# Edge attention on one core: the chain of maxima moved behind queries and sums in TensorE's order, scaling and merging one turn later

## What is computed

```python
k, q, v = ...                                   # per node, 4 heads of 64
score = sum(q_att[etype, col] * k[row], -1)     # per edge and head
m = segment_max(score, col)                     # over the edges into a node
ex = exp(score - m[col])
denom = segment_sum(ex, col)
agg = segment_sum(ex / denom[col] * msg[row], col)
```

## Time and profile before

| | us |
|---|---|
| median of 3 runs (7957.71 to 7974.63) | 7957.74 |
| the profiled execution | 7995.27 |
| its span | 7993.2 |
| mean granted PE clock, share of full | 0.75 |
| edge part of the first layer, first queries to last scaling | 816.8 to 2453.8 |
| edge part of the last layer, the same | 6073.4 to 7780.4 |

### The profile page before, as it was taken

The page is one execution under the profiler, slowest core; times in us unless marked ns, Lnnn a source line. Parts: engine busy times, 40 slices in busy tenths (PEclk is TensorE's granted clock), DMA queues, the critical chain, the costliest instruction groups (busy, mean ns, idle before and its releaser), DMA issues. The chain is left out here.

```text
span 7993.2 us, 97165 instructions
## 1 busy us (share of the span) xinstructions
PE 4632.6 (58%) x25691; PEld 3338.9 (42%) x25691; DVE 3629.8 (45%) x7669; ACT 2265.8 (28%) x7764; POOL 3116.6 (39%) x3162
## 2 busy tenths in 40 slices
PE   1698477777776404444445532885265666666664
PEld 1465355454455303333333322775122555555542
DVE  8111566666664341121111220111324878888875
ACT  0233355555453210000001110221011444444450
POOL 0320566666660026666662001001103555556540
PEclk9999677777778756666765556998566888888785
DMA  3333666666662223333333114872114666666662
GB/s 108 101 126 123 193 200 199 199 196 202 199 192 68 57 74 92 94 89 94 92 92 68 28 28 137 264 262 82 58 61 141 200 194 205 202 203 200 200 154 79
DMA packets 603761, 1110.04 MB, mean 139 GB/s; under 512 B 157032, under 2 KB 416238, under 8 KB 599843
## 3 DMA queue, kind: packets, MB, share of 16 engines
q0 software_dynamic: 204144, 617.42, 27.2%
q1 hardware_dynamic: 399216, 488.05, 18.9%
HBM read 983.67 MB, written 208.59 MB: 149 GB/s over the span
## 5 line engine op out<-in xcount | busy, mean ns | idle before, releaser
L714 POOL DMA_INDIRECT l3e_kv<-t_table,k_recs x912 | 966.7, 1060 | 706.9 <-ACT l3e_vw L991 385.7
L714 POOL DMA_INDIRECT l0e_kv<-t_table,k_recs x912 | 973.5, 1067 | 650.7 <-ACT l0e_vw L991 387.2
L1370 PE MATMUL l2e_pA<-l2e_row,l2e_oh 128*128 128x257 f32 x1824 | 614.9, 505 | 954.0 <-DVE l2e_acc L1349 329.3
L1324 POOL DMA_INDIRECT l2e_row<-t_table,l2e_idx x912 | 898.2, 985 | 403.7 <-issue 268.1
L1370 PEld LDWEIGHTS l2e_pA<-l2e_row,l2e_oh 128*128 128x128 f32 x1824 | 449.7, 255 | 1118.8 <-issue 1033.3
L948 PE MATMUL l0e_pA<-l0e_vw,l0e_ohf 128*128 128x260 f32 x1824 | 653.7, 499 | 197.6 <-issue 100.8
L991 ACT ACTIVATE l3e_vw<-l3e_kv,l3e_w 128x64 f32<-128x64 f32 x2736 | 679.8, 334 | 0.1
L991 ACT ACTIVATE l0e_vw<-l0e_kv,l0e_w 128x64 f32<-128x64 f32 x2736 | 679.8, 334 | 0.0
L900 PE MATMUL l3e_pQE<-l3e_qb,l3e_ohT 128*128 128x256 bf16 x2736 | 431.4, 320 | 405.6 <-issue 377.9
L1349 DVE SCALAR_TENSOR_TENSOR l2e_acc<-l2e_acc,k_itf,l2e_pA 128x257 f32<-128x257 f32 x228 | 109.8, 482 | 1065.4 <-issue 1000.8
L948 PEld LDWEIGHTS l0e_pA<-l0e_vw,l0e_ohf 128*128 128x128 f32 x1824 | 420.2, 244 | 353.7 <-issue 166.0
(11 more groups left out here) (452 smaller groups left out, 7541.6 us busy)
## 6 DMA issues: line engine op xcount, KB each, us to landing
exp_w<-in_L_gnn_w SPq DMA_DIRECT2D x224, 512.0 KB
t_table<-l0n_tab SPq DMA_DIRECT2D x26, 2048.0 KB, 6.8
l0e_qb<-t_q SPq DMA_DIRECT2D x228, 192.0 KB
l3e_qb<-t_q SPq DMA_DIRECT2D x228, 192.0 KB
t_agg<-l0e_acc SPq DMA_DIRECT2D x228, 130.0 KB
t_agg<-l3e_acc SPq DMA_DIRECT2D x228, 130.0 KB
l0e_drow<-t_drow SPq DMA_DIRECT2D x57, 512.0 KB
l3e_drow<-t_drow SPq DMA_DIRECT2D x57, 512.0 KB
```

Of the source, the lines that this page charges most:

```text
L714: pool.indirect_dma_start(kv[:, n % SK, g, :], None, table[:, :], bass.IndirectOffsetOnAxis(ap=K["recs"][:, n, g, ridx:ridx + 1], axis=0)) ...
L1324: pool.indirect_dma_start(row[:, s, g, 0:D], None, table[:, :], bass.IndirectOffsetOnAxis(ap=idx[:, i, g:g + 1], axis=0)).then_inc(row_rea ...
L1370: last = pe.matmul(pA[s % 2][:, 0:W], oh[:, s, g, :], row[:, s, g, :], start=(g == 0), stop=(g == G - 1))
```

## The change

On PE, `shift` goes from the head of turn j = 1 to its end, `spread` from turn j = 0 to turn j = 1 behind the queries, `turn_ends` behind the sums of turn j = 0. On DVE, `candidates`, `block_max` and `node_max` stand behind the merge of turn j = 1 and not ahead of its products; `shifted` and `drop_new` go from the end of turn j = 1 to the head of turn j = 2; scaling, rescaling and merging handle items one turn older (t - 2 and t - 4). ACT copies the turned ends at the head of turn j = 1 and not within the scaling of turn j = 0, and takes the exponentials in turn j = 2. PE sums item t - 3. SP stores item n - 13 behind the queries of n. Loops run one turn longer. No instruction is added or taken away.

```diff
-                n, r, x = t + BI, t - 3, t - 1
+                n, r, x = t + BI, t - 4, t - 2
...
-                if live(m) and j == 1:
-                    candidates(m)
-                    block_max(m)
+                if live(m) and j == 2:
+                    shifted(m)
+                    drop_new(m)
                 if 0 <= r < NI:
                     rescale(r)
-                if live(m) and j == 1:
-                    node_max(m)
...
                 if live(m) and j == 1:
-                    shifted(m)
-                    drop_new(m)
+                    candidates(m)
+                    block_max(m)
+                    node_max(m)
                 if n < NI:
                     scores(n)
+                if live(m) and j == 1:
+                    drop(m)
...
+                if n + 1 < NI:
+                    queries(n + 1)
+                if live(m) and j == 1:
+                    spread(m)
+                if 0 <= t - 3 < NI:
+                    sums(t - 3)
+                if live(m) and j == 0:
+                    turn_ends(m)
                 if live(m) and j == 1:
                     shift(m)
-                if n + 1 < NI:
-                    queries(n + 1)
-                if live(m) and j == 0:
-                    turn_ends(m)
-                    spread(m)
-                if 0 <= t - 2 < NI:
-                    sums(t - 2)
```

More of the change, by code:

```diff
@@ L686, in _ @@
             load_rows(1)
-            for n in range(1, NI + 12):
+            for n in range(1, NI + 13):
                 if n < NI:
@@ L988, in weigh @@
                     act.wait_ge(a_ps, n - VS + 1)
-                for g in range(g0, g1):
+                for g in range(AW):
                     for h in range(H):
                         last = act.activation(vw[:, v, g, h, 0:DK], kv[:, n % SK, g, D + h * DK:D + (h + 1) * DK], ACT.Copy, scale=w[:, m % 2, j, g, h:h + 1])
-                if g1 == AW:
-                    last.then_inc(vwa_ready, 1)
+                last.then_inc(vwa_ready, 1)
             def turned_ends(m):
@@ L1009, in weights @@
                 act.activation(w[:, m % 2, :, :, :].rearrange("p i g h -> p (i g h)"), z[:, :], ACT.Exp).then_inc(w_ready, 1)
-            for t in range(0, NI + 1):
+            for t in range(0, NI + 2):
                 m, j = divmod(t, BI)
-                y = t - 1
+                y = t - 2
                 if live(m) and j == 1:
+                    turned_ends(m)
+                if live(m) and j == 2:
                     weights(m)
```

16 lines of the change are left out of this document (5 added, 11 removed).

## The result

The changed kernel takes 8002.32 us (median of five runs, 7993.03 to 8027.22); the kernel before takes 7957.71 beside it. The ratio is 1.0053, 95% interval 1.0041 to 1.0064: 45 us slower by the medians, where 39 us faster was forecast. The time lies in the stated range (7700 to 8020), on the wrong side of its middle. The profiled execution took 8027.22 us, 32 more than the one of before.

What follows compares the result with a forecast made beforehand. The prediction took waits to bound the kernel, chiefly for PE completions released with POOL's gather runs. Last layer -46, first layer 0, ends +7 gave 7956 for the profiled execution, 7919 for the median; range 7700 to 8020.

Steps and rivals of the forecast that it cites:

- Late completions, released with POOL's run: Likeliest case: PE's completions stay late until POOL's gather run ends; 7919 us, between 7870 and 7945, chance 0.42.
- rival 2: The lateness is a backlog of PE's real work; 108 to 214 us saved, 7811 down to 7705, chance 0.22.
- Rival 3: Completions come on time in the new order and POOL bounds; 7565 us, with half of it 7740, chance 0.10.
- First layer at 0: First layer's batch stays 28.28 us, so no gain; bounds -6.2 to +1.7 us per batch.
- The waits merely move: First layer, DVE: the wait before `l0e_z` grows, the one before the merge goes, and the batch stays 28.28 us.
- `l0e_z` to the first freed slot stays 4.35: First layer: time from `l0e_z` until scaling frees a ring slot for POOL, taken as unchanged at 4.35 us.
- The forecast sign: First layer: `l0e_z` every 28 us or so, some 2.2 us behind POOL's last gather before a 6.5 us pause.
- Last layer at -0.8: Last layer: 0.8 us saved per batch, 57 batches, 46 us; bounds 86 us saved and 23 lost.
- the walk: Last layer, one batch step by step from `l3e_ohrT`'s end: best case 27.1 against 28.66 us, at worst 0.4 worse.
- The wrong sign the prediction named: Last layer: candidates waiting over 2.4 us, or a wait before `l3e_z`, would show the forecast wrong there.
- Ends at +7: One more turn at the end of each of the two edge parts, 3.38 us each, 7 us in all.
- Rival 4: First layer: lateness fixed per completion starts later, +1.7 us per batch; 8016 with the last layer's gain, 8062 without; chance 0.18.

Runs made afterwards that it cites:

- long pauses: Kernel before, with POOL writing a 128x1024 scratch tile between one item's gathers and the next's, first layer only; 7775 us on a late chip (one run).
- short pauses: POOL writes a 128x448 scratch tile between items' gathers, both layers: kernel before with it 7852 us (0.9868), changed kernel with it 7909 us (0.9941), late chips.
- the hold: POOL holds item 4m+8's gathers until batch m's spread completes: new order 1.0063, old order (first layer only) 1.0006 on the punctual chip, 1.0092 on late ones.
- the best order: New order in the first layer's edge part alone, last layer as in the kernel before; 7906 us, ratio 0.9943 on the late chips.

## Why the prediction was wrong, point by point

**Late completions, released with POOL's run: right in kind.** The prediction's first reading holds: before, `l0e_z` came within 3 us of the end of POOL's run in 39 of 40 batches, 2.2 us behind it in the median, and with pauses in POOL most of the lateness goes. PE's own backlog (rival 2) is refuted as its cause: the pauses take nothing from PE, and without gathers the same PE work is punctual. Rival 3 (punctual in the new order) fell with the first trace. A rival that the prediction doesn't name, that DVE itself is held back while POOL issues, has ACT's row at 1522.11 against it. Whether PE's array stands still in such a run or only its signals are held back is open; the ends of PE's rows are modelled. For the first speak the sums behind the shift in the kernel before, of the batch in the earlier trace rows, the first and the last row of eight matmuls:

```profile
1522.88 0.38 PE L948 MATMUL l0e_pA<-l0e_vw,l0e_ohf 128*128 128x260 f32 x1 [0.36 <-issue]
...
1527.83 1.03 PE L948 MATMUL l0e_pA<-l0e_vw,l0e_ohf 128*128 128x260 f32 x2 [1.30 <-issue]
```

They take 6.0 us, and over 3.9 in 38 of 41 batches, where eight take 1.9 in the median with long pauses. Against it: with short pauses they take 1.9 too, and `l0e_z` is still 5.6 us late. The Trainium skill, page "PSUM — Partial Sum Buffer", section "Engine vs sequencer instructions", says that an increment attached to the matmul fires on the instruction's completion; if so, the rows' ends are up to 8 us early on these chips. No run told the two apart.

**First layer at 0: mis-sized, -0.8 us per batch.** "The waits merely move" was right, but not one for one: 3.2 us before the merge and 1.8 before `l0e_z` became 4.0 before the candidates. The term that was off is "`l0e_z` to the first freed slot stays 4.35". In the new order DVE's scaling of the last item of the batch before stands between the candidates and `l0e_z`, and it frees the slot that POOL waits for (1547.45 and 1548.64 in the rows above). POOL restarts 0.85 us behind `l0e_z` in the median, and where the candidates end the wait, 3.4 behind them. So 21.75 + 2.18 + 4.35 became 22.04 + 1.86 + 3.43 = 27.3. The forecast sign, `l0e_z` some 2.2 us behind POOL's last gather and a pause of 6.5 us, came within 3 us in 12 of 40 batches only, and the pause was 5.3. From first to last `l0e_z` it is 35.4 us, inside the stated bounds.

**Last layer at -0.8: the step that failed.** Measured +1.1 (62.3 / 57) to +1.9 (30.59 - 28.72). The failed step is the walk's wait of 1.3 us before the candidates, with the spread's completion at 18.1: the spread was taken as punctual because in the earlier trace rows it was. It was so because POOL paused there; a turn's work moved ahead of it put it into POOL's run in 33 of 41 batches, where before it was 5, and there it is some 3 us late. In the other 8 the turned ends reach ACT late instead, by 5.5 us in the median (1.8 before), and the batch is no shorter. The wrong sign the prediction named, candidates waiting over 2.4 us, is what came (3.0).

The second half of the error is the comparison. The walk's 27.1 us is near what the new order takes where completions are punctual (26.9 with the hold). But it was set against 28.66, a batch of the old order with its late completions in it, and the old order too is shorter where they are punctual: 25.9. Set beside each other like this, the order seems to cost 0.7 to 1.0 us, though in each pair something else differs too, the hold or the chip. What of the order would cost that isn't settled: the wait of the relations for the key add, ahead of the spread, was the candidate, and taking it away won nothing on a late chip; on a punctual one it wasn't tried. And no run took the lateness away from the last layer on a late chip with the gathers kept, so how the loss splits between lateness and order is open.

The size of the term was a choice as well: the middle of the walk's -1.5 and +0.4 is -0.55, and -0.8 was taken.

**Ends at +7:** 5.2.

**The sum.** -46 + 0 + 7 was forecast, +62 - 35 + 5 came. Rival 4 had the time (8016) but not the place: it put the loss in the first layer, by lateness that is fixed per completion. The held POOL shows that it isn't fixed, since the candidates come 0.04 us behind the spread with it and 2.6 without; and the loss was in the last layer. That a rival's 8016 lies near the 8002 measured is luck.

## What to carry to other kernels

Compare a new order's best case with the old order's best case, not with its trace: a walk through queues gives times without the disturbances that the trace of the old one contains. Before moving a step, ask what made its completion punctual where it stood. And where completions trail their rows by microseconds while GpSimd issues gathers back to back, try short pauses in its stream before another order of the work: here the long ones won 2.2% (one run) and the short ones 1.3, where the best order won 0.6. That is for the late chips; on the punctual one, where POOL bounds the first layer, pauses weren't tried.

## What was not expected of the hardware

- Chips differ. The kernel before takes 7304.5 us on one chip and 7950 to 7960 on three others, at mean granted clocks of 0.78 and 0.76. In the first layer PE's completions are punctual there (0.04 us in the old order with the hold) under an unbroken stream of gathers (POOL: 222 us idle for 729 gathers, nearly all of it the gaps of 0.30). The stretch between the two edge parts is shorter there too: 3526 us with the hold, against 3705 of the kernel before on a late chip. What sets these chips apart isn't known.
- More work sped the kernel up: four writes of 0.97 us by POOL took 3.4 us off a batch of 28.3, and half as long ones 2.0.
- Lateness at `l0e_z` does not follow the bytes in flight (198 or 123 GB/s: 8.1 us both). With 16 records instead of 128 it shifts from there to the candidates (2.8 and 6.7 us), and the batch is no shorter.
